# DLRM tower on one core: a mix of its own for the first chunk

## The reference

```
z[b, ij] = sum over e, f of  e_i[b, e] * param[f, ij, e] * e_j[b, f]
h = relu(concat(z, dense_ctx) @ W_top1 + b_top1)     # 796 -> 512
h = relu(h @ W_top2 + b_top2)                        # 512 -> 256
y = h @ W_top3                                       # 256 -> 1
```

## Time and profile before

| | |
|---|---|
| the runs, median | 1220.51 us |
| the profiled execution | 1219.68 us |
| its span, first to last instruction | 1217.9 us |
| TensorE, VectorE, ScalarE, GpSimd busy | 98%, 89%, 79%, 48% of the span |
| granted TensorE clock | 1.00 in every stretch |

### The profile page before, as it was taken

One profiled execution on the slowest core, in us unless ns is written; L12 is line 12 of the kernel. 1 busy time (PEld: TensorE's weight loads), 2 busy tenths in 40 slices (PEclk: granted clock), 3 DMA queues, 4 the chain that ended last, 5 costly groups with the idle time before them and its releaser, 6 DMA issues.

```text
span 1217.9 us, 21902 instructions
## 1 busy us (share of the span) xinstructions
PE 1191.0 (98%) x5772; PEld 426.8 (35%) x5772; DVE 1081.9 (89%) x970; ACT 957.0 (79%) x7341; POOL 582.5 (48%) x623
## 2 busy tenths in 40 slices
PE   8989999998999999999999999999999999999999
PEld 2323333332333333333333334333333333333323
DVE  8589999998998888899998889899999888889990
ACT  6459979997678967899866976999877896789872
POOL 6766766566655545666243546666515452000000
DMA  4224332222332222222222222222222222111100
GB/s 117 51 69 145 78 76 75 73 66 66 76 74 65 55 61 64 69 72 68 63 70 56 63 54 66 73 67 75 73 52 74 58 61 57 37 52 44 53 10 1
DMA packets 50717, 78.45 MB, mean 64 GB/s; under 512 B 13800, under 2 KB 14056, under 8 KB 50464
## 3 DMA queue, kind: packets, MB, share of 16 engines
q1 hardware_dynamic: 30872, 56.81, 16.0%
q0 software_dynamic: 19712, 20.22, 8.5%
q10 hardware_dynamic: 8, 0.01, 0.0%
HBM read 76.98 MB, written 0.01 MB: 63 GB/s over the span
## 4 chain that ended last, share of the span: by engine, by line
PE 86%; ACT 6%; DVE 5%; issue 3%; DMA 0%; SPq 0%; DVEq 0%; ACTq 0%
PE ring L709 29%; PE ring L715 23%; PE z_ps L728 15%; PE aux L626 6%; ACT act_prod L488 6%; PE aux L674 3%; PE aux L664 2%; PE ring L626 2%; DVE prod L618 2%; PE aux L633 2%; DVE sums L559 1%; DVE act_prod L618 1%; DVE dve_prod L618 1%; PE aux L640 1%; PE ring L633 1%
## 5 line engine op out<-in xcount | busy, mean ns | idle before, releaser
L488 ACT ACTIVATE act_prod<-act_prod 128x64 f32<-128x64 f32 x3584 | 856.6, 245 | 65.2 <-DVE act_prod L618 64.9
L488 ACT ACTIVATION_READ_ACCUMULATOR act_prod<-act_prod 128x1 f32 x3584 | 685.3, 191 | 0.0
L618 DVE TENSOR_TENSOR prod<-ring,emb 128x1024 f32<-128x1024 f32 x448 | 517.3, 1213 | 48.5 <-PE ring L710 48.2
L439 POOL DMA_INDIRECT stage<-tbl,idx x384 | 362.5, 944 | 309.9 <-PE aux L674 139.8
L709 PE MATMUL ring<-emb,raw 64*128 64x512 f32 x896 | 436.8, 608 | 14.0 <-DVE prod L618 4.4
L710 PE MATMUL ring<-emb,raw 64*128 64x512 f32 x896 | 437.0, 609 | 0.0
L715 PE MATMUL ring<-raw,emb 64*128 64x512 f32 x704 | 360.3, 619 | 2.8 <-issue 1.5
L716 PE MATMUL ring<-raw,emb 64*128 64x512 f32 x704 | 360.4, 620 | 0.0
L618 DVE TENSOR_TENSOR act_prod<-ring,kept 128x1024 f32<-128x1024 f32 x224 | 262.7, 1213 | 35.7 <-PE ring L716 34.9
L439 POOL DMA_INDIRECT kept<-tbl,idx x232 | 219.2, 945 | 130.6 <-issue 100.5
L709 PEld LDWEIGHTS ring<-emb,raw 64*128 64x128 f32 x896 | 153.4, 186 | 240.9 <-issue 137.1
(11 more groups left out here) (51 smaller groups left out, 331.7 us busy)
## 6 DMA issues: line engine op xcount, KB each, us to landing
raw<-param_b SPq DMA_DIRECT2D x200, 256.0 KB, 2.7
stage<-tbl,idx POOLq DMA_INDIRECT x384
kept<-tbl,idx POOLq DMA_INDIRECT x232, 2.5
W<-W1g SPq DMA_DIRECT2D x1, 1792.0 KB, 7.3
act_prod<-tbl SPq DMA_DIRECT2D x6, 224.0 KB
W<-W2t SPq DMA_DIRECT2D x1, 512.0 KB, 9.5
idx<-ids_t SPq DMA_DIRECT2D x1, 240.0 KB, 5.7
act_prod<-tbl SPq DMA_DIRECT2D x6, 26.0 KB
```

The source lines that it names most:

```text
L439: pool.indirect_dma_start(to[:, t, E * (f % 2) : E * (f % 2) + E], None, tables[f], bass.IndirectOffsetOnAxis(ap=idx[:, c, f, t : t + 1], ...
L488: op = act.activation(part, part, ACT.Copy, accum_out=sums[:, t, at : at + 1])
L618: dve.tensor_tensor(to, ring[:, n % RING, :, :], by, ALU.mult).then_inc(prod_done, 1)
```

## The change

The plan's lists become a class `Chunk`, and chunk 0 gets an object of its own. Its mix is 30 batches by fields and 20 by samples; VectorE sums 6 of the 20, ScalarE 14 as before. Chunks 1 to 3 have the lists they had.

```diff
+class Chunk:
+    def __init__(self, second, dve_sums, early, late):
+        self.samples = [(m, 0) for m in range(SIDE, DUOS)] + [(m, 1) for m in range(second, DUOS)]
...
+KINDS = [
+    Chunk(second=16, dve_sums=[1, 5, 8, 11, 15, 18], early=2, late=18),
+    Chunk(second=14, dve_sums=[1, 4, 7, 9, 12, 15, 18, 20], early=2, late=18),
+]
+KIND_OF = [0, 1, 1, 1]
```

```diff
-                sp.dma_start(raw[:, n % RAW, :], param_b[n % NB]).then_inc(raw_loaded[n % RAW], 16)
+                sp.dma_start(raw[:, n % RAW, :], param_b[NB * KIND_OF[n // NB] + n % NB]).then_inc(raw_loaded[n % RAW], 16)
...
             def load_dense(c):
-                sp.wait_ge(z_saved, FGROUPS * (c + 1))
+                tenant = z_tenant(c, "samples", SGROUPS - 1)
+                if tenant >= 0:
+                    sp.wait_ge(aux_ready, AUX_NO["h1", tenant, H1 // P - 1] + 1)
+                else:
+                    sp.wait_ge(aux_ready, AUX_NO["duo", 0, HOT[-1]] + 1)
...
-                if n >= NB and n % NB == RAW + 1:
-                    load_dense(n // NB - 1)
-            load_dense(NCH - 1)
+                if n % NB == LAYER_BATCHES[-1]:
+                    load_dense(n // NB)
+                if n == NB + LAYER_BATCHES[-1]:
+                    sp.wait_ge(aux_ready, AUX_NO["h1", 0, H1 // P - 1] + 1)
+                    sp.dma_start(W1[:], W1g[1]).then_inc(next_W1_loaded, 16)
...
-                    act.activation(z[:, z_place(c, "samples", n), :], aux[:], ACT.Copy).then_inc(aux_saved, 1)
+                    rows = DENSE_ROW if n == SGROUPS - 1 else P
+                    act.activation(z[0:rows, z_place(c, "samples", n), :], aux[0:rows, :], ACT.Copy).then_inc(aux_saved, 1)
...
                         pe.wait_ge(dense_loaded, 16 * (c + 1))
+                        if c:
+                            pe.wait_ge(next_W1_loaded, 16)
```

More of the change, by code:

```diff
@@ L47 @@
 SIDE = ROWS // 2
-SECOND = 14
 BATCH = 4
[L52 to L73, removed]
-NU = BATCH * NB
-AT = {x: n for n, x in enumerate(BATCHES)}
-assert NU == 200 and NF * BATCH == len(FIELD_UNITS)
+NB = FIELDS * FIELDS // 32
+NU = BATCH * NB
+class Chunk:
+    def __init__(self, second, dve_sums, early, late):
+        self.samples = [(m, 0) for m in range(SIDE, DUOS)] + [(m, 1) for m in range(second, DUOS)]
+        self.samples.sort()
+        self.field_units = []
+        for m in range(DUOS):
+            done = [d for x, h in self.samples if x == m for d in ROW_DUOS[h]]
+            self.field_units += [("full", m, k) for k in range(m) if k not in done]
+            if m % 2:
+                self.field_units.append(("diag", m - 1, m))
+        self.nf = len(self.field_units) // BATCH
+        self.ns = len(self.samples)
+        self.dve_sums = dve_sums
+        self.act_sums = [i for i in range(self.ns) if i not in dve_sums]
+        self.batches = []
+        made = 0
+        for j in range(self.nf):
+            self.batches.append(("fields", j))
+            while made < self.ns and (made < early if j == 1 else made * (self.nf - 2) < self.ns * j - late):
+                self.batches.append(("samples", made))
+                made += 1
+        self.at = {x: n for n, x in enumerate(self.batches)}
+        assert len(self.batches) == NB and made == self.ns and self.batches[-1][0] == "fields"
+        self.first = {}
+        self.last = {}
+        for u in range(NU):
+            kind, x = self.batches[u // BATCH]
+            used = self.field_units[BATCH * x + u % BATCH][1:] if kind == "fields" else self.samples[x][:1]
+            for d in used:
+                self.last[d] = u
+            for d in range(max(used) + 1):
+                self.first.setdefault(d, u)
@@ L78 @@
+KINDS = [
[3 more added lines that the diff above has]
+KIND_OF = [0, 1, 1, 1]
+CHUNKS = [KINDS[x] for x in KIND_OF]
+FIELDS_BEFORE = [sum(x.nf for x in CHUNKS[:c]) for c in range(NCH)]
 QUADS = BATCH // 2
@@ L80 @@
 GROUP_BATCHES = SLOTS // QUADS
-FGROUPS = -(-NF // GROUP_BATCHES)
-SGROUPS = -(-NS * 2 * ROWS // P)
+FGROUPS = 4
+SGROUPS = 3
 PER_GROUP = P // (2 * ROWS)
@@ L87 @@
 GROUP_NO = {x: n for n, x in enumerate(GROUPS)}
-assert NG == FGROUPS + SGROUPS
-DENSE_ROW = 2 * (NF * QUADS - (FGROUPS - 1) * SLOTS)
-assert DENSE_ROW + DENSE <= 32
+DENSE_ROW = P - DENSE
+for _kind in KINDS:
+    assert -(-_kind.nf // GROUP_BATCHES) == FGROUPS and P * (SGROUPS - 1) < 2 * ROWS * _kind.ns <= P * SGROUPS - DENSE
 SUM_PLACES = 2
@@ L105 @@
 FIRST_LEAD = 4
[L108 to L121, removed]
 SUM_AT = {}
 for _c in range(NCH):
-    for _b, (_kind, _x) in enumerate(BATCHES):
-        if _kind == "fields" and (_c, _x) != (NCH - 1, NF - 1):
-            _next = BATCHES[(_b + 1) % NB][0]
+    for _b, (_kind, _x) in enumerate(CHUNKS[_c].batches):
+        if _kind == "fields" and (_c, _x) != (NCH - 1, CHUNKS[_c].nf - 1):
+            _next = CHUNKS[_c].batches[(_b + 1) % NB][0]
             SUM_AT[NU * _c + BATCH * _b + (6 if _next == "samples" else 5)] = (_c, _x)
@@ L140 @@
 _at = -TURN
-_early = min(FIRST[_d] - TURN * _d for _d in range(DUOS))
 for _c in range(NCH):
+    _first = CHUNKS[_c].first
+    _early = min(_first[_d] - TURN * _d for _d in range(DUOS))
     for _d in range(DUOS):
         _at = max(_at + TURN - 1, NU * _c + TURN * _d + _early - (LEAD if _c else FIRST_LEAD))
-        _at = max(0, min(_at, NU * _c + FIRST[_d]))
+        _at = max(0, min(_at, NU * _c + _first[_d]))
         DUO_AT[_c, _d] = _at
-        if _at < NU * _c + FIRST[_d] - 4:
+        if _at < NU * _c + _first[_d] - 4:
             DUO_AT[_c, _d] = next((_at + u for u in (0, 1, -1, 2, -2, 3) if apart(_at + u)), _at)
@@ L175 @@
     _c, _u = divmod(_n, NU)
-    _kind, _x = BATCHES[_u // BATCH]
-    if _kind == "samples" and _x in DVE_SUMS:
+    _kind, _x = CHUNKS[_c].batches[_u // BATCH]
+    if _kind == "samples" and _x in CHUNKS[_c].dve_sums:
         _waiting.append((_c, _x, _u % BATCH))
@@ L189 @@
 for _c in range(NCH):
-    for _i in ACT_SUMS:
+    for _i in CHUNKS[_c].act_sums:
         for _t in range(BATCH):
-            _at = max(_at + 3, 4 * (NB * _c + AT["samples", _i] + 1) + 2 * _t + SLACK)
+            _at = max(_at + 3, 4 * (NB * _c + CHUNKS[_c].at["samples", _i] + 1) + 2 * _t + SLACK)
             ACT_AT.setdefault(_at // 4, []).append((_c, _i, _t))
@@ L217 @@
         FREED[_c, _d] = _until[_n] if _free else None
-        _until[_n : _n + 1] = [NU * _c + max(LAST[_d], LAST[_d + 1])]
+        _until[_n : _n + 1] = [NU * _c + max(CHUNKS[_c].last[_d], CHUNKS[_c].last[_d + 1])]
         PLACE[_c, _d], PLACE[_c, _d + 1] = 2 * _n, 2 * _n + 1
@@ L347, in sampled, with dve_group_end, act_group_end, field_prod @@
         def sampled(c, i, t):
[L348 to L352, removed]
+            if i in CHUNKS[c].dve_sums:
+                return BT * (sum(len(x.dve_sums) for x in CHUNKS[:c]) + CHUNKS[c].dve_sums.index(i)) + t
+            return BT * (sum(len(x.act_sums) for x in CHUNKS[:c]) + CHUNKS[c].act_sums.index(i)) + t
+        def dve_group_end(c, g):
+            mine = sum(1 for i in CHUNKS[c].dve_sums if i < PER_GROUP * (g + 1))
+            return BT * (sum(len(x.dve_sums) for x in CHUNKS[:c]) + mine)
+        def act_group_end(c, g):
+            mine = sum(1 for i in CHUNKS[c].act_sums if i < PER_GROUP * (g + 1))
+            return BT * (sum(len(x.act_sums) for x in CHUNKS[:c]) + mine)
+        def field_prod(c, j, t):
+            return prod[:, (BATCH * (FIELDS_BEFORE[c] + j) + t) % PROD, :, :]
         def sums_place(c, g):
@@ L533, in _ @@
             act.wait_ge(stored, 16 * last)
-            act.activation(z[:, z_place(last, "samples", SGROUPS - 1), :], aux[:], ACT.Copy).then_inc(tail_saved, 1)
+            act.activation(
+                z[0:DENSE_ROW, z_place(last, "samples", SGROUPS - 1), :], aux[0:DENSE_ROW, :], ACT.Copy
+            ).then_inc(tail_saved, 1)
             for m in range(H1 // P):
@@ L594, in _ @@
                 c, u = divmod(n, NU)
-                kind, x = BATCHES[u // BATCH]
+                kind, x = CHUNKS[c].batches[u // BATCH]
                 t = u % BATCH
@@ L699, in make_unit @@
                     pe.wait_ge(raw_loaded[at % RAW], 16 * (at // RAW + 1))
-                newest = max([d for d in range(DUOS) if FIRST[d] == u], default=0)
+                newest = max([d for d in range(DUOS) if CHUNKS[c].first[d] == u], default=0)
                 if newest:
@@ L729, in sum_batch @@
                             z_ps[32 * q : 32 * q + 32, :], sel[:, 30 - 2 * slot : 62 - 2 * slot],
[L730 to L731 removed]
+                            field_prod(c, j, 2 * i + q // 2)[:, q % 2, :],
+                            start=(slot == 0), stop=(slot == SLOTS - 1 or (j == CHUNKS[c].nf - 1 and i == QUADS - 1)),
                         )
[L733 removed]
+                if j % GROUP_BATCHES == GROUP_BATCHES - 1 or j == CHUNKS[c].nf - 1:
                     mm.then_inc(group_summed, 1)
@@ L758, in _ @@
                 elif m == 1:
-                    sum_batch(last, NF - 1)
```

(12 more changed lines are left out.)

48 lines of the change are left out of this document (24 added, 24 removed).

## The result

The changed kernel takes 1212.83 us (median of four runs, 1212.48 to 1213.39) against 1220.34 before: ratio 0.9938, 95% interval 0.992 to 0.9955. It is faster by 7.5 us, where 5.9 was forecast (1214.6). The profiled execution took 1213.15, its span is 1211.4 against 1217.9, so the two traces differ by 6.5 us, and that is what can be explained from them; the last microsecond of 7.5 lies between runs.

A forecast was written before the change was run, and what follows sets the result against it. VectorE was taken to bound chunk 0 (262.4 us against TensorE's 247.4), TensorE the later chunks. Terms -9.05 +4.9 +1.5 -3.2 = -5.85 took 1219.68 to 1213.8; plus 0.83 for the median, 1214.6, range 1208.3 to 1218.8.

The forecast's parts named there:

- the stretch: Chunk 0 from product 28 to product 228 on VectorE, 268.5 us before; all forecast terms lie here, -5.85 us.
- Eight reduces: VectorE in chunk 0: 32 reduces become 24, at 1.131 us each, with nothing to hide them: -9.05 us.
- The stall at the turn: Gap at 281.33, TensorE waiting for ScalarE's save of turned sums; goes as the turn moves from unit 174 to 185: -3.2 us.
- Rival B: ScalarE stays late and the 3.16 us stall returns at another unit: -2.65 us, so 1217.9; chance 0.14.
- Duo 10: Turned at unit 38, the first that uses it, instead of 41: new early wait at product 38, +1.5 us.
- Six bare sums and the one behind a turn: TensorE sums without a reduce beside them: gaps of 0.6 to 1.1 us, and 0.3 at 187, +4.9 us.
- rival C: Sums without a reduce beside them cost their whole 2.05 us: +4.7 us, so 1225.2; chance 0.05.
- rival A: Full cover: ring and ScalarE's slack hide all, leaving -9.05 and -3.2, so 1208.3; chance 0.10.
- W1's second load and the dense rows: 1792 KB load behind weights 91, and last dense rows loaded earlier: no weights late, nothing saved, 0 us.
- Rival D: Second W1 load blocks raw weights, landing 10 us after issue; undoing the gain needs 19.5: 1220.5 or more; chance 0.04.
- The gain holds to the end: From product 228 on, chunks 1 to 3 keep their old plan and length, so chunk 0's gain stays.
- VectorE's busy share from 100 to 300 us: Sign to look for: the share falls from full to about 97%.

The follow-up runs named there:

- all sums bare: Changed kernel with chunk 0's VectorE reduces two units behind the sums, so no sum has a reduce beside it: 1228.88 us.
- the disturbed chip: Chip that ran every kernel about 400 us longer; there the changed kernel with chunk 0's old 28/22 mix had ratio 1.0001 to the kernel before.
- 29/21: Changed kernel with chunk 0 at 29 batches by fields, 21 by samples, seven of these summed by VectorE: 1213.31 us, ratio 0.994 to the kernel before.
- the early duos: Changed kernel with three duos turned sooner, at units 29, 35 and 208: 1211.51 us, ratio 0.9928 to the kernel before.

## Why the prediction was right

The forecast for the stretch was -5.85 us, measured is -6.2. By its steps:

- *Eight reduces, -9.05.* Right: VectorE's busy time fell by 9.0, and with eight reduces back in the new mix the stretch is 268.3 again.
- *The stall at the turn, -3.2.* Right, and shown alone: 2.9 in the stretch with nothing else of chunk 0 changed. Rival B falls, but by less than forecast: the save came at 293.9, not at 290.5, and ended 1.3 us before the bank was wanted, not 6. ScalarE began the seven tiles 1.5 later than reckoned (263.7 for 262.2), and at 269.97 it had idled 2.30 us for the transposes of a duo, which the reckoning left out; it had one save less to make (0.5). That the stall went is the mechanism as forecast, that so thin a margin held is luck.
- *Duo 10, +1.5.* Measured 1.04, at product 38 as forecast. (The two times of the forecast, 101.3 and 99.6, give 1.7 and not 1.6.) The sum before it came at 95.93 for 96.4, and from the duo's transposes to the product 2.5 us passed, not 2.87.
- *Six bare sums and the one behind a turn, +4.9.* Each at the product forecast: 0.75, 0.75, 1.00, 0.75, 0.99 and 1.27, and 0.26 at 187, 5.8 in all. Each costs 0.08 more, since the instruction before a gap takes its full 1.21 and not 1.13; 6.3. This term was 1.4 too small. The run with all sums bare bears out the mechanism, a lead of limited length: 0.75 or 0.82 at 19 of 30, and nothing to speak of where a reduce stood two or three units before, where rival C had 2.05 and rival A nothing. The figure of 2.3 us for the lead is an estimate; no run measures it.
- *What the sum left out.* The small delays of before, 1.5 us in seven places, were carried over as they were. They stood behind reduces, and 0.2 is left of them in the changed kernel; why they went was not tested. This hid the error of the term above: -9.05 - 3.2 + 1.1 + 6.3 - 1.3 = -6.15. That the sum came within 0.3 of the measured stretch is in part luck.
- *W1's second load and the dense rows, 0.* Right: the load is issued at 534.5 and lands 9.5 us after (7.8 to 10.8 in the other kernels, those of the disturbed chip left aside); products 400 to 600 take 288.9 in both kernels. Rival D falls; its landing forecast (10 us for the raw weights behind it) is not seen in the trace, only that nobody waited. A save of 112 rows took 597 to 601 ns, one of 128 rows 573 to 600.
- *The gain holds to the end.* Right, to 0.1 us per chunk.
- *VectorE's busy share from 100 to 300 us.* It fell from 98.0% to 97.5%. The forecast's 97% is near, but the share was not full before.

Where the prediction was poorer is in what it took the change to be. It took the 30/20 mix as the step that pays. The runs show that 29/21 pays as much, that the second batch swapped only trades four reduces (4.5 us) and 1.7 us of small delays for five more bare sums (5.1 us together) and an early duo (1.1 with its 0.08), and that nearly half of the gain could be had by moving one turn.

## What to carry to other kernels

When two engines pass tiles through a short ring, their totals set only the floor. What one engine does beside the stream (here a sum of 2 us) is free if the other has work of its own at that very place or just before, and costs the ring's shortfall (here 0.75 to 1.27) if not; the reduces of one chunk moved back by two units cost 15.7 us. And before a mix is changed to relieve an engine, look for the single long gap in it: here 3.2 us stood at one wait for a bank, and its cure was to move the use that waited.

## What the runs showed of the hardware that was not expected

A bare sum that stands alone, with a unit by samples behind it, costs the same 0.75 us in four different plans (products 43 and 51 above, 43 in the mix with eight reduces, 43 with the early duos, 127 among others in the kernel with all sums bare).

And long waits cost TensorE more than themselves. In the kernel with the new mix in all chunks TensorE stood still from 391.8 to 397.8 us, the wait of 6.01 above. Stretches of 2 us, as in the earlier trace rows:

```profile
392.00:394.00 2.00, 0.00 (x0) 0.00 (x0) 1.43 (x2) 2.00 (x19) 1.51 (x2) 1.00 0.62 167
394.00:396.00 2.00, 0.00 (x0) 0.00 (x0) 0.00 (x0) 2.00 (x19) 1.58 (x2) 0.57 0.18 32
...
398.00:400.00 2.00, 2.00 (x3) 0.97 (x4) 0.00 (x0) 0.00 (x0) 1.16 (x2) 0.50 0.00 0
...
404.00:406.00 2.00, 2.00 (x7) 0.71 (x7) 0.00 (x0) 0.24 (x1) 1.42 (x2) 1.00 0.17 27
```

The granted clock fell to 0.50, 1.2 instead of 2.4 GHz, while the engine stood still, and was at 1.00 again from 402 us on. In between the layer's matmuls went at about half their pace, 3 in 2 us for 7 later. A wait of 4.79 us before 436.19 did the same. The wait of 2.98 us in the kernel before left the clock at 1.00.
